# Macaron layer on one core: two places for the pieces of each recurrent step, LayerNorm sums on VectorE, one key product on GpSimd

## The reference

```python
def ffn(x):                       # x: (T=8, 1024 rows, 256), scan over T
    def step(c, xt):
        ft = sigmoid(xt @ wf.T + c @ uf.T + bf)
        it = sigmoid(xt @ wi.T + c @ ui.T + bi)
        gt = tanh(xt @ wc.T + c @ uc.T + bc)
        return ft * c + it * gt, None
    c, _ = scan(step, c0, x)
    return tanh(einsum('tbi,oi->tbo', x, wo) + c @ uo.T + bo)

def attn(x):                      # gated delta rule over L=1024, 16 heads of 16
    s = x @ W.T
    k = q = rmsnorm(x per head) * k_norm_w
    # per token: S = lam*S; S += beta * k (x) (v - k^T S); o = q^T S,  with v = -s
    return layernorm(s + o) * w + b

x = x + 0.5 * ffn(layernorm(x))
x = x + attn(layernorm(x))
x = x + 0.5 * ffn(layernorm(x))
```

## Time and profile before

| | |
|---|---|
| median of 3 runs | 1659.71 us (1651.63 to 1661.19) |
| profiled execution | 1644.96 us |
| its span, first to last instruction | 1643.1 us |
| busy: PE, DVE, ACT, POOL | 1407.7, 901.5, 743.8, 149.3 us |
| mean granted clock of TensorE | 0.922 |
| chain that ended last | PE 61%, DVE 17%, ACT 12%, issue 8% |

### The profile page before, as it was taken

How to read it: one execution, slowest core, us unless ns; L and a number is a source line. 1 busy time by engine, 2 the same in 40 slices (tenths; PEclk the granted TensorE clock), 3 DMA queues, 4 the chain that set the end, 5 groups by cost and what they waited for, 6 DMA issues and landing times.

```text
span 1643.1 us, 61959 instructions
## 1 busy us (share of the span) xinstructions
PE 1407.7 (86%) x27811; PEld 1294.4 (79%) x27811; DVE 901.5 (55%) x2104; ACT 743.8 (45%) x1841; POOL 149.3 (9%) x198
## 2 busy tenths in 40 slices
PE   5889888888988988888878878878889999998887
PEld 4888877787877877777677767868888989898876
DVE  2555866756667465447744864573434545454522
ACT  4565553543635544444443444344335444454342
POOL 0000000000000000001200120030040404040400
PEclk9999998998988988899798989879989999999999
DMA  3011111202111232223123221321422424242100
GB/s 122 1 52 53 54 54 66 93 29 80 55 54 55 80 111 63 86 82 109 52 94 112 88 86 45 121 86 50 155 77 87 123 80 131 74 134 64 42 27 26
DMA packets 56649, 125.39 MB, mean 76 GB/s; under 512 B 10944, under 2 KB 31680, under 8 KB 52288
## 3 DMA queue, kind: packets, MB, share of 16 engines
q1 hardware_dynamic: 56384, 121.42, 22.6%
HBM read 62.13 MB, written 59.24 MB: 74 GB/s over the span
## 4 chain that ended last, share of the span: by engine, by line
PE 61%; DVE 17%; ACT 12%; issue 8%; DVEq 0%; ACTq 0%
PE ps L451 31%; PE ps L998 6%; PE ps L820 5%; PE ps L518 5%; PE ps L652 4%; PE ps L982 3%; ACT gates L468 3%; PE ps L676 2%; DVE ln_bn L119 2%; ACT ffn_rows L137 2%; ACT inv_cols L776 2%; ACT gates L475 1%; PE ps L411 1%; ACT zbd L1020 1%; DVE prod L745 1%
## 5 line engine op out<-in xcount | busy, mean ns | idle before, releaser
L451 PE MATMUL ps<-cst,wt 128*128 128x128 f32 x2688 | 363.5, 292 | 9.9 <-DVE cst L496 9.0
L451 PEld LDWEIGHTS ps<-cst,wt 128*128 128x128 f32 x2688 | 336.4, 203 | 20.1 <-DVE cst L496 10.0
L451 PE MATMUL ps<-ffn_rows,wt 128*128 128x128 f32 x2304 | 297.8, 289 | 18.3 <-ACT gates L468 5.9
L451 PEld LDWEIGHTS ps<-ffn_rows,wt 128*128 128x128 f32 x2304 | 285.0, 203 | 25.8 <-ACT ffn_rows L420 7.9
L490 DVE TENSOR_TENSOR fc<-gates,cst 128x256 f32<-128x256 f32 x112 | 51.6, 461 | 360.5 <-ACT gates L468 360.2
L468 ACT ACTIVATE gates<-ps,colv 128x128 f32<-128x128 f32 x448 | 127.4, 366 | 223.6 <-PE ps L451 223.5
L1087 POOL TENSOR_TENSOR ffn_rows<-ffn_rows,rowv 128x256 f32<-128x256 f32 x64 | 53.6, 872 | 1271.3 <-DMA ffn_rows<-x_scratch 1271.3
L998 PE MATMUL ps<-e,kgb 32*128 32x64 f32 x4032 | 130.4, 276 | 10.0 <-ACT e L1007 6.6
L820 PE MATMUL ps<-inv_cols,kv 32*32 32x32 f32 x8192 | 93.3, 201 | 51.2 <-issue 32.0
L998 PEld LDWEIGHTS ps<-e,kgb 32*128 32x128 f32 x4032 | 121.7, 189 | 19.0 <-issue 13.4
L820 PEld LDWEIGHTS ps<-inv_cols,kv 32*32 32x32 f32 x8192 | 84.6, 112 | 63.5 <-issue 44.3
(11 more groups left out here) (125 smaller groups left out, 1800.6 us busy)
## 6 DMA issues: line engine op xcount, KB each, us to landing
kg_scratch<-kg_rows SPq DMA_DIRECT2D x8, 2048.0 KB, 8.3
xs_scratch<-xs_out SPq DMA_DIRECT2D x16, 1024.0 KB, 4.4
xsb<-xs_scratch SPq DMA_DIRECT2D x64, 256.0 KB, 3.4
kgb<-kg_scratch SPq DMA_DIRECT2D x256, 64.0 KB, 2.7
ffn_rows<-x SPq DMA_DIRECT2D x8, 1024.0 KB, 5.2
x_scratch<-ffn_rows SPq DMA_DIRECT2D x8, 1024.0 KB, 4.5
e_scratch<-e SPq DMA_DIRECT2D x256, 32.0 KB, 1.8
ffn_rows<-e_scratch SPq DMA_DIRECT2D x8, 1024.0 KB, 6.8
```

What stands on the lines that cost most here:

```text
L451: mm = pe.matmul(banks[g][:, col:col + P], wt[:, w, k, m * P:(m + 1) * P], rhs, start=(x in (0, FI)), stop=(k == KT - 1 and (t == 0 or x > ...
```

## The change

2. Where the two places are. In blocks 0 to 5:

```diff
 def first_pe(pe):
-    ff.pe_step(pe, b, t, 0, NX)
-    ff.pe_step(pe, b, t, NX, 2 * NX)
-    pieces(pe, b, t, prep_pe, solve_pe)
+    ff.pe_step(pe, b, t, 0, FI)                 # 8 gate products of the input
+    pieces(pe, b, PERIOD[t][0], prep_pe, solve_pe)
+    ff.pe_step(pe, b, t, FI, 2 * NX)            # 4 candidate products, 12 of the state
+    pieces(pe, b, PERIOD[t][1], prep_pe, solve_pe)
     ff.pe_h(pe, b, 0)
-    gram_pe(pe, b.n - 1, 2)
+    pieces(pe, b, LAST_GRAM, prep_pe, solve_pe)
     ff.pe_h(pe, b, 1)
+    pieces(pe, b, LAST_UNIT, prep_pe, solve_pe)
 def first_act(act):                             # first_dve alike, with dve_step
+    pieces(act, b, PERIOD[t][0], prep_act, solve_act)
     ff.act_step(act, b, t)
-    pieces(act, b, t, prep_act, solve_act)
+    pieces(act, b, PERIOD[t][1], prep_act, solve_act)
```

From step 48 on, ACT, DVE and POOL take both lists one behind the other where the one list stood; on PE:

```diff
 def second_pe(pe):
-    f.pe_step(pe, b, t + 1, 0, NX)
-    pieces(pe, *period_of(i), prep_pe, solve_pe)
+    f.pe_step(pe, b, t + 1, 0, FI)
+    pieces(pe, *period_of(i, 0), prep_pe, solve_pe)
+    f.pe_step(pe, b, t + 1, FI, NX)
+    # t == 7: f.pe_h(pe, b, 0)
+    pieces(pe, *period_of(i, 1), prep_pe, solve_pe)
+    # t == 7: pe_h 1, LAST_GRAM, front fills 0 and 1 of the next block, LAST_UNIT, cterm
-    # t == 7: pe_h 0, g2, front fill 0, pe_h 1, front fill 1, cterm
```

4. The keys:

```diff
 elif name == "keys":                            # DVE
-    dve.tensor_tensor(kv_of(n)[:, :, 0:HD], by_head(key_rows), by_lane(r_lam), ALU.mult)
-    dve.tensor_tensor(kg_rows...[:, :, 0:HD], by_head(key_rows), by_lane(r_g), ALU.mult)
-    dve.tensor_tensor(by_head(key_rows), by_head(key_rows), by_lane(rms), ALU.mult)
+    dve.tensor_tensor(by_head(key_rows), by_head(key_rows), rms..., ALU.mult)
+    dve.tensor_tensor(kv_of(n)..., key_rows..., lam_tok..., ALU.mult)
+def prep_pool(pool, n, name):                   # POOL, at the second place of step 5
+    wait_pos(pool, kg_out, 16 * n)
+    pool.wait_ge(key_done, KEY_OPS * n + 1)
+    for r in range(KG_OPS):                     # 4 operations of 512 elements
+        pool.tensor_tensor(kg_rows...[2 * r], key_rows...[2 * r], g_tok..., ALU.mult)
```

244 lines of the change are left out of this document (110 added, 134 removed), and 8 rows, old and new, of the table PERIOD.

## The result

| | before | changed |
|---|---|---|
| median of 10 runs each, taken together | 1653.20 us | 1666.07 us (1661.85 to 1680.25) |
| ratio of the two, 95% interval | 1 | 1.0094 [1.0062, 1.0126] |
| profiled execution | 1644.96 us | 1664.46 us |
| its span, mean granted clock | 1643.1 us, 0.922 | 1662.7 us, 0.920 |

What follows compares the result with a forecast made beforehand. TensorE was taken as the bound, busy 1407.7 us of 1643.1. The terms -78 + 77 + 32 = +31 us gave 1676 for the profiled execution, 1691 on the runs' scale; own range 1676 to 1712, 80% range 1630 to 1722.

Steps and rivals of the forecast that it cites:

- +77: Blocks 0 to 5: sum of new waits, with ACT and DVE taking first-place pieces before the step's work; +77 us.
- -78: Whole kernel: sum of waits removed, mostly for ACT or DVE to empty PSUM banks, some for issue; -78 us.
- `g0`, `g1`: Blocks 1 to 5, step 7: g0 is emptied late behind ln1 and ap0, PE waits at g1; 6.0 us each, 30.
- `gt1`: Blocks 2 to 5: PE waits for gt0's banks, emptied only behind ln2; 3.3 us, 4.6 in block 2, 14.5 in all.
- `lt0`: Block 1: it stands ahead of the recurrent products but waits for eight applied tiles; 2.6 us.
- Sum +32: Blocks 6 to 15: all new waits that the change adds there; +32 us.
- the copy of e behind `ta4`: Hop blocks: ACT, held at ta4 by the store, copies e late; 2.35 us in three blocks, 7 us.
- `ln1` before the state copies: Block 6: ln1, 5.8 us on DVE behind km0, delays the hop's state copies; 4 us.
- `rms` beside GpSimd: Blocks 6 to 15: the delay by rms moves from tt to ta0; 3.3 us in two blocks, 6.6.
- It balances: Rival, blocks 0 to 5: half of the new waits hide behind others or issue waits; 1652 us, chance 0.22.
- The lower clock follows: Rival: waits at g1 and 3 us waits bring half speed, POOL costs two turns; +63, 1722 us, chance 0.08.
- That GpSimd costs: Step 6: POOL's key work contends with DVE's products, taken as 1.45 us; with free interfaces the sum is 7 us less.

Runs made afterwards that it cites:

- e1: Changed kernel with ap0 moved in step 7 from ahead of g0 to the second place, behind g1; 0.9948 of the kernel before.
- e8: e1 with the unit outputs' first half stored ahead of x1 and the first front fill between the first output products (blocks 10 to 14); 0.9866 of the kernel before.
- a third place: Both kernels with step 3's 12 input products in block 0 made three times, shifting TensorE's later instructions; changed / before 1.0009.
- e4: Changed kernel with the four kg products on DVE, behind the normalising product, in place of GpSimd; 1.0066 of the kernel before.
- e3: Changed kernel, but in blocks 6 to 15 TensorE makes all 12 input products of the next step before both lists of pieces; 1.0241 of the kernel before.
- e6: e1, but in blocks 0 to 5 every engine takes both lists of pieces behind the whole step; 1.0052 of the kernel before.

## Why the prediction was right in direction and wrong in size

**Blocks 0 to 5, right in sum.** The terms gave +77 there. Of the -78, 43 or so are waits that lie there in the kernel before: +34. Measured: 9.1 + 28.2 = +37.3. That the sum came so near is partly luck, since its parts were less good:
- `g0`, `g1`: the mechanism was right, but at the second gram it is 4.0 us in blocks 3 to 5, 2.45 in block 2 and none in block 1, where 6.0 were forecast for each; the waits of the grams come to 20.0 us in blocks 1 to 5, where 30 were forecast. e1 shows its cost, 7.6 us of length in blocks 1 to 5.
- Block 0, 5 forecast: 5.31 us of waiting, but 9.1 of length. With e1's edit it is gone. Its other half is the clock: PE was busy 4.9 us longer in block 0, where I had put the clock at zero.
- `tt0` 2.5 us in each of blocks 2 to 5 (2.3 forecast) and `kt0` 1.7 to 2.2 (2.2): right.
- `gt1`: 3.3 forecast, 0.75 in block 4, 5.7 in all for 14.5. The timeline of PE and DVE there:

```profile
401.75 1.05 PE L423 MATMUL ps<-ffn_rows,wt 128*128 128x128 f32 x8 [1.71 <-issue]
...
406.79 0.17 DVE L95 SCALAR_TENSOR_TENSOR ln_stats<-ln_bn,ln_stats 128x8 f32<-128x8 f32 x1
...
408.02 0.69 PE L782 MATMUL ps<-ident,key_rows 128*128 128x128 f32 x4 [0.75 <-DVE inv L719]
```

  Step 0 starts at S = 393.16. DVE ended `ln2` at S+13.8, as forecast (S+14.0); but PE, forecast at `gt1` by S+12.3, came at S+14.1, since it had stood 1.71 us for issue.
- `lt0`: 2.6 us in block 1 forecast, 15.1 in blocks 1 to 5 measured. I had worked out that the xs store holds ACT at `ta4`, and applied it only to the copies of e in the hop blocks. In blocks 3 to 5 it held the apply of `ln2`; e8 shows it.

**Blocks 6 to 15, the step that failed.** I had put +32 of new waits against some 35 removed: about -3. Measured: -23.8 + 6.0 = -17.8. The failed step is the "Sum +32": of its terms, 28.8 us belong to blocks 6 to 9, and about 6 us of them are found there:
- the waits other than for issue fell there by 23.9 us, new ones included (54.0 to 30.1), so most of the 35 was indeed removed;
- the copy of e behind `ta4`: 7 forecast; L985 waits 4.1 us in all, where L998 before waited 6.6, and none of the four stands behind `ta4`. e8, which takes the hold away, leaves these blocks as they were;
- `ln1` before the state copies: 4 forecast, none seen. `v01`: 4.4 forecast, 1.2. `rms` beside GpSimd: 6.6 forecast, and one wait of 1.74 us, at `ta0` of block 7, where `rms` held up a state copy of DVE. `tt1` and `gt1`: 3.8 forecast, none for a bank;
- `ta3` behind `g2`: 3 forecast, 1.46 and 1.51 measured, right.

The likely reason, argued and not tested: I had costed each by the lateness of the engine that delivers, one at a time, without asking whether PE itself would be late by then. In these blocks PE has 2600 to 3100 matmuls per block, and 46 us of issue waits stand between the pieces; what was to be 1.5 to 2.4 us late was mostly there when PE came. In blocks 10 to 15 6.0 us were lost for 3.5 forecast, with a clock of 0.96 in place of 0.97.

**The scale.** The forecast for the profiled execution was 1676, and it was 1664.5: 11.5 us too much; the step above alone would be 15, and blocks 0 to 5 gave back 3. The other half of the 25 us is in going from it to the median. The runs shown had a median 0.9% above the profiled execution; in the comparison the kernel before had 1653.2, 0.5% above it, and the changed kernel's median, 1666.1, was 0.1% above its own. One profiled execution says no more about a median than these tenths. And part of even the measured 0.94% may be the stream's position, since a third place left 0.1 to 0.2%.

**The signs.** Block 1 grew to 85.4 us (about 85 said), with `ap0` just before `g0`, and the second gram waited 4.0 us, in three blocks of five. The gram's transposes (now L782) wait over 2 us only in block 2 (4.21), not in blocks 2 to 5; no wait for e follows `ta4`, and DVE's products beside GpSimd are not slowed.

**Rivals.** "It balances" (1652, by half of the new waits hiding) came nearest in kind, but it had them hide in blocks 0 to 5; they hid in the hop blocks. "The lower clock follows" was wrong for the sum (0.920 for 0.922), right for block 0. That GpSimd costs was a term of 7 us; e4 shows none. Its source was read too widely: the row of 0.77 us in the earlier trace rows is an operation with one input, which takes 0.23 us elsewhere, and only the row behind it has one with two inputs, 0.71 us for the 0.29 of the same line later:

```profile
947.73 0.71 DVE L61 TENSOR_TENSOR hs<-rms 128x128 f32<-128x128 f32 x1
```

So small operations are held, but a long product of DVE keeps its 2.29 us, and GpSimd is held.

**Still open.** Which of the waits for issue in blocks 6 to 9 are owed to the place of the stream and which to the pieces' order (42.0 us before, 46.0 after) is not settled; the third place at which both kernels are equal doesn't exclude that this part is all of the difference. That `ln1` on DVE costs by itself was not tried alone; e1's block 0 (83.0 us at its end, 83.4 before) says that it needs not. Also open is what the two places by themselves gain: e3 and e6, which take them back, lose by waits for issue, and each at one position of the stream.

## To carry to other kernels

When one engine is the bound, cost a piece's place by all the queues that it passes through: the same name stands in the lists of PE, ACT, DVE and SyncE, and here a layer norm's apply in front of a bank's reading (1.5%), transposes in front of the recurrent products (0.6%, its interval reaching none) and a store behind another store (0.8%, with the fronts) cost together more than the rest of the change gained. A new wait of the busiest engine counts only if that engine is on time when it gets there, and then the clock can add most of its length again (4.2 us on 5.74 here). Before a difference under one percent is put down to an edit, shift the whole instruction stream and measure again.

## What the hardware did that was not expected

- **A wait costs more than itself.** After 5.74 us of waiting 8 transposes took 1.97 us; with the engine busy in that time, 1.09. Filling the wait with useless products made block 1 6.8 us shorter, 2.6 of it by issue waits that went too.
- **Instruction supply has places.** The same 64 matmuls of a hop stop behind the first of them for 4.97 us in two kernels that reach them 33 us apart, and 32 matmuls earlier in a third whose stream is 96 matmuls shorter: 256 instructions apart, counted with the weight loads. Such waits come to about 63 us of the kernel before and 71 us of the changed one.
- **A move of the stream alone changes the time**: of e1's version by 1.1% (5 us of it are work), of its blocks 6 to 9 by 22 us. The kernel before moved by -0.34% and +0.07%, hardly beyond its intervals, but its block 6 by up to 13 us.
- **GpSimd gives way to a long VectorE product.** Its product of 512 elements took 1.06 us at the median and up to 3.16 us beside a DVE product, which kept its 2.29 us.
- **A store holds its source for long**: 7.9 us from issue until ACT could write, issued half a us behind the x1 store, in place of the 4.4 us to landing of the earlier trace rows.
